# GpSimd takes over one of the two input products of each state step in a fused Mamba, MoE and attention kernel

## The reference

```python
u, z  = split(x @ W_in.T)                       # 256 channels each
uc    = silu(conv3(u) + conv_b)
proj  = uc @ W_xproj.T
B, C, dt = proj[..., :16], proj[..., 16:32], proj[..., 32:]
delta = softplus(dt @ W_dt.T + b_dt)            # per position and channel
for t in positions:                             # state of 256 channels x 16
    h = exp(delta[t] * A) * h + (delta[t] * uc[t]) * B[t]
    y[t] = sum over the 16 states of h * C[t]
out = ((y + uc * D) * silu(z)) @ W_out.T
```

## Time and profile before

| | |
|---|---|
| median of 3 runs | 2798.36 us (2792.71 to 2799.37) |
| the profiled execution, its own time | 2799.84 us |
| its span, first to last instruction | 2797.7 us |
| busy share of the span | PE 77%, DVE 75%, ACT 63%, POOL 55% |
| granted TensorE clock, mean | 0.890 |
| state steps of sequences 0 to 3 | 77 to 905 us of the span |

### The profile page before, as it was taken

One profiled execution on the slowest core, in us unless ns is written; L12 is line 12 of the kernel. 1 busy time (PEld: TensorE's weight loads), 2 busy tenths in 40 slices (PEclk: granted clock), 3 DMA queues, 4 the chain that ended last, 5 costly groups with the idle time before them and its releaser, 6 DMA issues.

```text
span 2797.7 us, 42437 instructions
## 1 busy us (share of the span) xinstructions
PE 2156.8 (77%) x15570; PEld 1468.6 (52%) x15570; DVE 2095.7 (75%) x3549; ACT 1751.3 (63%) x2757; POOL 1549.5 (55%) x1375
## 2 busy tenths in 40 slices
PE   2333787588499597988889898889995798839876
PEld 1101455356266474655666566556664568636665
DVE  3999889789888215999999999999998432572344
ACT  5444776686565546988888888888894234212422
POOL 0435433533533103878877887898788424563146
PEclk8555898799599798999999999999998899859988
DMA  3000000000000000000000010110010000000000
GB/s 109 0 0 0 1 1 1 1 1 1 19 1 1 16 8 23 24 24 24 24 24 24 24 27 23 31 26 24 24 35 24 1 1 1 1 16 1 1 1 16
DMA packets 32032, 42.05 MB, mean 15 GB/s; under 512 B 8897, under 2 KB 18130, under 8 KB 31442
## 3 DMA queue, kind: packets, MB, share of 16 engines
q1 hardware_dynamic: 31826, 39.34, 5.2%
HBM read 12.05 MB, written 2.10 MB: 5 GB/s over the span
## 4 chain that ended last, share of the span: by engine, by line
PE 35%; DVE 29%; ACT 12%; issue 11%; POOL 11%; SPq 0%; DMA 0%; POOLq 0%; ACTq 0%; DVEq 0%
DVE MA L1329 12%; PE ps L891 6%; DVE WB L1338 5%; PE ps L820 3%; POOL MA L429 3%; ACT HR L792 2%; PE ps L1161 2%; PE ps L822 2%; PE ps L821 2%; PE ps L1190 2%; PE ps L2020 2%; ACT BIG L463 2%; PE ps L1173 2%; PE ps L1962 1%; ACT L792 1%
## 5 line engine op out<-in xcount | busy, mean ns | idle before, releaser
L1329 DVE TENSOR_REDUCE MA<-ps 128x1 f32<-128x1024 f32 x512 | 606.6, 1216 | 46.4 <-PE ps L1161 42.5
L1257 ACT ACTIVATE WB<-ps,MA 128x1024 f32<-128x1024 f32 x461 | 513.8, 1118 | 105.5 <-DVE MA L1329 93.3
L429 POOL TENSOR_TENSOR MA<-MA,BIG 128x1024 f32<-128x1024 f32 x128 | 303.0, 2389 | 495.2 <-DVE BIG L355 470.7
L1161 PE MATMUL ps<-BIG 96*128 96x512 f16 x1024 | 315.9, 391 | 98.9 <-ACT WB L1257 87.5
L1413 POOL TENSOR_SCALAR WB<-WB,MA 128x384 f32<-128x384 f32 x256 | 371.1, 1450 | 8.5
L891 PEld LDWEIGHTS ps<-WB,HR 128*128 128x128 f32 x2304 | 279.0, 195 | 27.4 <-issue 11.6
L891 PE MATMUL ps<-WB,HR 128*128 128x128 f32 x2304 | 286.0, 280 | 7.2 <-DVE acc L727 7.2
L792 ACT ACTIVATE HR<-ps,b 128x512 f32<-128x512 f32 x288 | 190.3, 687 | 127.6 <-PE ps L822 126.6
L1767 POOL TENSOR_TENSOR BIG<-MA,BIG 128x512 f32<-128x512 f32 x128 | 133.0, 1048 | 229.5 <-PE ps L2006 76.1
L1173 PE MATMUL ps<-ident,WB 128*128 128x128 f32 x1640 | 223.8, 280 | 9.8 <-DVE WB L1338 5.6
L1416 POOL TENSOR_TENSOR WB<-WB 128x384 f32<-128x384 f32 x205 | 208.9, 1019 | 17.1
(11 more groups left out here) (300 smaller groups left out, 4968.3 us busy)
## 6 DMA issues: line engine op xcount, KB each, us to landing
BIG<-BIG SPq DMA_DIRECT2D x192, 64.0 KB, 2.0
BIG<-MA SPq DMA_DIRECT2D x192, 64.0 KB, 2.0
WB<-w_dram SPq DMA_DIRECT2D x1, 2304.0 KB, 14.7
X<-x_dram SPq DMA_DIRECT2D x4, 512.0 KB, 12.4
HR<-w_dram SPq DMA_DIRECT2D x1, 2048.0 KB, 9.4
out_dram<-X SPq DMA_DIRECT2D x4, 512.0 KB, 3.2
BIG<-wqkv_dram SPq DMA_DIRECT2D x1, 1536.0 KB, 6.2
WB<-w_dram SPq DMA_DIRECT2D x2, 512.0 KB, 4.9
```

The lines of the kernel that those rows point to most:

```text
L429: e.tensor_tensor(yy[:, c, :], yy[:, c, :], db[n % 2][c], ALU.add).then_inc(*p_my.up(b, n, c))
L1161: x = e.matmul(ps[s][:, 512 * h:512 * h + 512], stack[q % 2][0:96, 0, 2 * pp + s, 128 * i:128 * i + 128], stack[q % 2][0:96, 1, 2 * pp + s ...
L1257: e.activation(P_of(n, s), ps[s][:, :], ACT.Exp, bias=L[:, 2 * s + pp:2 * s + pp + 1], scale=1.0, accum_out=L[:, 4 + 2 * s + pp:5 + 2 * s ...
L1329: e.tensor_reduce(L_of(n)[:, c:c + 1], ps[s][:, :], AX, ALU.max, negate=True).then_inc(*v_amx.up(n, s))
```

## The change

Half 0's input product leaves DVE and goes to POOL (inputs_pool), which can't read PSUM, so the row of B is brought by a transfer instead: ACT's queue writes the 16 rows of B from the tile projected to DRAM once per sequence (b_rows), and SP's queue loads row n, spread over 128 partitions (rows_sp), right into db[k][0], where the product is then made in place. scan0 waits for POOL's product (p_mtb), scan1 as before for DVE's. Half 1, both scans, the products with C and POOL's adds stay. The rows0 matmuls stay too, for half 1. DVE's first softplus operation waits for the write of the rows (its output overwrites projected), du of the next sequence waits for POOL's last product of the sequence before. The loads of the attention's weights stand behind rows_sp in SP's queue. Several semaphores are merged into one each (a_mfront, v_mfront) without another order of events, and all planned positions are set anew. Those that the prediction uses, besides LOOP_AT: N_PERIOD 13.11 to 13.1; IN_AT (position in the steps of the sequence before) conv0 92.1 to 96.3, sp0 138.3 to 138.2, dl0 149.4 to 149.5, sp1 161.6 to 161.2, dl1 176.9 to 176.8, stats 61.3 to 61.4 (POOL's scale_shift 2.5 behind it), du 200.1 to 200.

```diff
 LOOP_AT = {"tb": -0.76, "scan1": 2.84, "scan0": 4.1, "th": 7.79, "add": 10.18, ...}     # before
 LOOP_AT = {"tb": -2.59, "scan1": 2.76, "scan0": 5.14, "th": 8.02, "add": 10.55, ..., "tb0": -1.13}  # after
...
         def loop_dve(e, b):
             for n in range(16):
                 k = n % 2
                 yield l_at(b, n, LOOP_AT["tb"])
                 e.wait_ge(*t_mrow[0].at(b, n))
-                for c in range(2):
-                    if n >= 2:
-                        e.wait_ge(*p_my.at(b, n - 2, c))
-                    elif b:
-                        e.wait_ge(*p_my.at(b - 1, 14 + n, c))
-                    e.tensor_tensor(db[k][0] if c == 0 else ps[0][:, :], du[:, c, :], ps[0][:, :], ALU.mult).then_inc(
-                        *v_mtb.up(b, n, c))
+                if n >= 2:
+                    e.wait_ge(*p_my.at(b, n - 2, 1))
+                elif b:
+                    e.wait_ge(*p_my.at(b - 1, 14 + n, 1))
+                e.tensor_tensor(ps[0][:, :], du[:, 1, :], ps[0][:, :], ALU.mult).then_inc(*v_mtb.up(b, n))
                 for c in (1, 0):
                     yield l_at(b, n, LOOP_AT[f"scan{c}"])
                     e.wait_ge(*a_mda.at(b, n, c))
-                    e.wait_ge(*v_mtb.at(b, n, c))
+                    e.wait_ge(*(v_mtb.at(b, n) if c else p_mtb.at(b, n)))
...
+        def inputs_pool(e, b):
+            for n in range(16):
+                yield l_at(b, n, LOOP_AT["tb0"])
+                if n == 0:
+                    e.wait_ge(*v_mtb.at(b, "du"))
+                e.wait_ge(s_bcast[n % 2], 16 * (8 * b + n // 2 + 1))
+                e.tensor_tensor(db[n % 2][0], du[:, 0, :], db[n % 2][0], ALU.mult).then_inc(*p_mtb.up(b, n))
+
+        def rows_sp(e):
+
+            for b in range(NB):
+                e.wait_ge(s_brow, 16 * b + 16)
+                for n in range(16):
+                    if n >= 2:
+                        e.wait_ge(*p_my.at(b, n - 2, 0))
+                    elif b:
+                        e.wait_ge(*p_my.at(b - 1, 14 + n, 0))
+                    e.dma_start(db[n % 2][0], b_dram[b, n:n + 1, :].partition_broadcast(128)).then_inc(s_bcast[n % 2], 16)
...
+            yield in_at(b, "wx", 4.2)
+            e.wait_ge(*a_m.at("wx", b, 1))
+            e.dma_start(b_dram[b, :, :], projected[64:80, :]).then_inc(s_brow, 16)
...
             for c in range(2):
                 yield in_at(b, f"sp{c}")
-                e.wait_ge(*a_mexp.at(b, c))
-                if c:
-                    e.wait_ge(*v_mdl.at(b, 0))
+                e.wait_ge(*a_mfront.at(b, "exp", c))
+                if c == 0:
+                    e.wait_ge(s_brow, 16 * b + 16)
+                else:
+                    e.wait_ge(*v_mfront.at(b, "dl", 0))
...
             yield in_at(b, "du")
+            if b:
+                e.wait_ge(*p_mtb.at(b - 1, 15))
             for c in range(2):
-                e.wait_ge(*v_mdl.at(b, c))
-                e.tensor_tensor(du[:, c, :], dl[b % 2][:, c, :], uc[:, c, :], ALU.mult).then_inc(*dve_own.up())
+                e.wait_ge(*v_mfront.at(b, "dl", c))
+                i = e.tensor_tensor(du[:, c, :], dl[b % 2][:, c, :], uc[:, c, :], ALU.mult)
+                i.then_inc(*(v_mtb.up(b, "du") if c == 0 else dve_own.up()))
...
         @block.gpsimd
-            weave(over(loop_pool, e), over(front_pool, e), over(back_pool, e), over(moe_pool, e),
+            weave(over(loop_pool, e), over(inputs_pool, e), over(front_pool, e), over(back_pool, e), over(moe_pool, e),
...
         @block.sync
         def _(e):
             load(e)
+            rows_sp(e)
             attention_sp(e)
```

More of the change, by code:

```diff
@@ L84, in keys @@
     return out
-N_PERIOD, M_PERIOD, M_FIRST = 13.11, 209.76, 56.0
+N_PERIOD, M_PERIOD, M_FIRST = 13.1, 209.6, 56.0
 PLAN = [(h, e) for h in range(2) for e in (8, 0, 1, 2, 3, 4, 5, 6, 7)]
 WEIGHTED = []
-IN_AT0 = {"stats": -0.58, "norm": 1.89, "tr": 7.85, "u": 12.93, "tap0": 16.6, "tap1": 15.13, "conv0": 14.42,
-          "conv1": 22.1, "silu": 21.6, "wx": 23.8, "bc1": 26.4, "bc2": 27.8, "wdt0": 29.5, "wdt1": 35, "exp": 36.6,
-          "sp0": 40.2, "ln0": 39, "dl0": 42.9, "sp1": 40.1, "ln1": 49.1, "dl1": 51.2, "du": 52.2}
@@ L93 @@
[L93 to L104, removed]
@@ L105 @@
-F_AT3 = {"stats": -0.54, "norm": 3.84, "tr": 1.58, "flo": 14.87, "gate": 11.29, "top": 11.76, "e": 15.6, "wts": 9.85,
-         "cT": 19.46, "k": 13.36, "K": 6.65, "up": 1.05, "dn": 12.94, "dnj": 0.67, "ge": 0.43, "done": -0.33,
-         "add": 7.21, "end": 136.6, "rnorm": 137.1, "x": 135.5}
+IN_AT0 = {"stats": -1.25, "norm": 1.77, "tr": 7.53, "u": 13.01, "tap0": 16.77, "tap1": 12.45, "conv0": 14.68,
+          "conv1": 21.9, "silu": 19.41, "wx": 24.5, "bc1": 28.2, "bc2": 27.5, "wdt0": 29.5, "wdt1": 35.9,
+          "exp": 36.6, "sp0": 40, "ln0": 50.4, "dl0": 43.8, "sp1": 35.7, "ln1": 48.3, "dl1": 50.3, "du": 51.9}
@@ new lines @@
+IN_AT = {"stats": 61.4, "norm": 68.4, "tr": 75, "u": 80.1, "tap0": 89.9, "tap1": 91, "conv0": 96.3, "conv1": 86.7,
+         "silu": 96.6, "wx": 101.5, "bc1": 109, "bc2": 121, "wdt0": 107.6, "wdt1": 126.6, "exp": 135.9, "sp0": 138.2,
+         "ln0": 142.6, "dl0": 149.5, "sp1": 161.2, "ln1": 169.9, "dl1": 176.8, "du": 200}
+OUT_AT = {"gate": 6.92, "yy": 6.94, "out": 11.16, "stats": 18.56, "rstd": 21.2, "norm": 33.2, "x": 35.2}
+OUT_AT3 = {"gate": 1.22, "yy": 7.14, "out": 5.72, "stats": 7.8, "rstd": 19.15, "norm": 13.22, "x": 22.4}
@@ new lines @@
+F_AT0 = {"stats": -2.31, "norm": 5.53, "tr": 6.58, "flo": 8.97, "gate": 10.05, "top": 17.5, "e": 15.83, "wts": 11.99,
+         "cT": 25.8, "k": 17.92, "K": 8.73, "up": 0.87, "dn": 3.66, "dnj": 1.45, "ge": 1.19, "done": 11.03,
+         "add": 8.31, "end": 181.3, "rnorm": 190.6, "x": 186.4}
+F_AT2 = {"stats": 3.93, "norm": 2.49, "tr": 6.54, "flo": 14.29, "gate": 18.14, "top": 23.4, "e": 24, "wts": 26.6,
+         "cT": 26.5, "k": 17.67, "K": 8.28, "up": 0.65, "dn": 6.97, "dnj": 0.23, "ge": 0.92, "done": 11.15,
+         "add": 8.32, "end": 176, "rnorm": 170.2, "x": 179.4}
@@ L108 @@
+F_AT3 = {"stats": -0.61, "norm": 1.25, "tr": 1.84, "flo": 15.09, "gate": 11.25, "top": 10.63, "e": 15.89,
+         "wts": 10.09, "cT": 19.39, "k": 13.36, "K": 6.65, "up": 1.04, "dn": 7.56, "dnj": 0.57, "ge": 0.46,
+         "done": -0.09, "add": 6.98, "end": 137.5, "rnorm": 137.1, "x": 135.6}
 F_AT = [F_AT0, F_AT0, F_AT2, F_AT3]
-LOOP_AT = {"tb": -0.76, "scan1": 2.84, "scan0": 4.1, "th": 7.79, "add": 10.18, "da": -0.17, "rows0": 5.17,
-           "rows1": 13.83, "z": 18.68, "zK": -4.54, "za": 4.8}
@@ L111 @@
-A_AT = {"norm0": 10.66, "norm1": -0.24, "norm2": 10.19, "turn": 9.1, "op": 15.77, "opK": 2.47, "ope": 0.85,
-        "v": 36.5, "vK": -3.75, "lam": -12.29}
+LOOP_AT = {"tb": -2.59, "scan1": 2.76, "scan0": 5.14, "th": 8.02, "add": 10.55, "da": 0.03, "rows0": 5.28,
+           "rows1": 13.84, "z": 19.93, "zK": -1.57, "za": 6.24, "tb0": -1.13}
+A_AT = {"norm0": 10.44, "norm1": -0.26, "norm2": 8.64, "turn": 8.51, "op": 15.77, "opK": 2.47, "ope": 1.65,
+        "v": 40.8, "vK": -5.27, "lam": -12.29}
@@ L235, in program @@
             path[p], user[n] = (x, user.get(n)), p
-        a_muc, a_mexp, a_mlog, a_mda = tick("a_muc", NB, 2), tick("a_mexp", NB, 2), tick("a_mlog", NB, 2), tick("a_mda", NB, 16, (1, 0))
-        a_myy, a_mtap = tick("a_myy", NB, 2), tick("a_mtap", NB, 2)
+        a_mfront, a_mda = tick("a_mfront", NB, ("tap", "silu", "exp", "log"), 2), tick("a_mda", NB, 16, (1, 0))
+        a_myy = tick("a_myy", NB, 2)
         t_mrow = {k: tick(f"t_mrow{k}", NB, 16) for k in range(2)}
@@ L241, in program @@
         v_mst, a_mln, p_mrs = (Tick(sem(x), m_order) for x in ("v_mst", "a_mln", "p_mrs"))
-        v_mconv, v_mbc, v_mu1, v_mdl = tick("v_mconv", NB, 2), tick("v_mbc", NB), tick("v_mu1", NB, 2), tick("v_mdl", NB, 2)
-        v_mtb, v_mscan, v_mth = tick("v_mtb", NB, 16, 2), tick("v_mscan", NB, 16, (1, 0)), tick("v_mth", NB, 16, (1, 0))
+        v_mfront = Tick(sem("v_mfront"), [(b, x, c) for b in range(NB) for x, c in (("conv", 0), ("conv", 1), ("bc", 0), ("u1", 0), ("dl", 0),
+                                                                                ("u1", 1), ("dl", 1))])
+        v_mtb, v_mscan, v_mth = tick("v_mtb", NB, ("du", *range(16))), tick("v_mscan", NB, 16, (1, 0)), tick("v_mth", NB, 16, (1, 0))
         v_mgate = tick("v_mgate", NB, 2)
+        p_mtb, s_brow, s_bcast = tick("p_mtb", NB, 16), sem("s_brow"), [sem(f"s_bcast{k}") for k in range(2)]
+        b_dram = nc.dram_tensor("b_rows", (NB, 16, 1024), F32, kind="Internal").ap()
         p_my, p_mx = tick("p_my", NB, 16, (1, 0)), tick("p_mx", NB)
@@ L515, in front_act @@
                 e.wait_ge(*a_m.at("wdt", b, c, 1))
-                e.activation(ee[c], ee[c], ACT.Exp, bias=0.0, scale=-1.0).then_inc(*a_mexp.up(b, c))
+                e.activation(ee[c], ee[c], ACT.Exp, bias=0.0, scale=-1.0).then_inc(*a_mfront.up(b, "exp", c))
             for c in range(2):
                 yield in_at(b, f"ln{c}")
-                e.wait_ge(*v_mu1.at(b, c))
```

(3 more changed lines are left out.)

34 lines of the change are left out of this document (17 added, 17 removed).

## The result

The changed kernel takes 2838.54 us (median of 4, 2833.55 to 2847.33) against 2798.02 (median of 4, 2792.71 to 2799.37): a ratio of 1.0156, with the interval 1.014 to 1.0172. It is 40 us slower. The forecast was 2815 in a range that ends at 2838: slower, as forecast, but by more than twice as much, and just outside the range.

A forecast was written before the change was run, and what follows sets the result against it. DVE was taken to bound sequence 0's steps, the experts on PE and ACT to set the pace in the other stages. 2799.84 + 18.0 - 1.1 + 0 = 2816.7 us, against the median 2815; range 2777 to 2838.

The forecast's parts named there:

- Bare periods: Steps without other work, in sequence 0: from 9.08 us to 10.54 us each, 1.46 us longer.
- the sum for sequence 0: Sequence 0's 16 periods, taken one by one: plus 18.0 us, hidden by nothing.
- the ring: Between DVE and POOL: th, two adds, next step's product, scan0, th again, waiting on each other, 10.54 us a step.
- Two engines at one port: DVE operations with two SBUF inputs and POOL operations go one after the other; without it, 3 us less in sequence 0.
- Loads: Row loads of 512 KB, write of 64 KB and later attention weights: all hidden, cost 0.
- Stages of sequences 1 to 3: Steps beside the experts: gains and losses cancel, 0 taken, with -18 and +8 us as ends for each.
- Outside of it I reckon ... 0 to +2: Sequences 1 to 3, periods outside PE's and ACT's chain: 0 to +2 us per stage.
- The +1 for gate and statistics: Sequences 1 to 3: gate and back statistics, 2.3 us each, lie behind scan0; +1 us per stage.
- The other moved positions ... 3 us to either side: Remaining moved positions and merged semaphores, not priced from rows: 3 us to either side.
- The rival with the dearer port: Front and back two-input operations wait for whole POOL operations in sequences 1 to 3: 8 us a stage, 2839; 0.08 together with late loads.
- Freed DVE time is worth nothing where PE and ACT carry the chain: Sequences 1 to 3, periods of 13 to 22 us: a DVE done sooner just waits longer for PE.
- The rival with 54 us to come back: Freed DVE time returns in the three expert stages: two thirds, 36 us, gives 2779; chance 0.27.

The follow-up runs named there:

- the port alone: Kernel before, plus one extra POOL product per step of sequence 0, behind the two adds, that no step waits for: sequence 0 takes 188.4 us.
- old positions: Changed kernel with all planned positions of the kernel before: 2835.8 us, ratio 1.0138 to the kernel before.
- the run with steps 8 to 14: Kernel before's positions, with POOL making half 0's product only in steps 8 to 14 of sequences 1 to 3: 2797.02 us, ratio 0.9997.
- the last version: Kernel before, with POOL's product ahead of the adds and a third buffer in sequence 0's steps 1, 3, 6, 10, and later convolution there: 2796.57 us, ratio 0.9995.
- the run with the third buffer: Changed kernel with a third buffer for half 0 in sequence 0 and the next step's product ahead of the adds: 2818.9 us.

## Why the prediction was right and wrong

- **Bare periods and the sum for sequence 0**: right. 10.54 us, and 188.9 - 170.8 = 18.1 for the stage against 18.0; the first scan0 1.7 us earlier against 1.1. Most parts are right within a microsecond: the statistics period 13.28 (13.1), sp0 12.42 (12.4), dl1 12.92 (12.9), convolution 14.95 (15.6), the B and C pairs in the gap 12.06 and 11.89 (11.7). Two errors cancel: sp1 (offset 161.2) stands ahead of scan0 of step 12 and so in dl0's period, which takes 14.28 us, and leaves the next one bare, 10.53; I had 12.9 and 11.7. du has the right number, 12.87 (12.8), for another reason: it isn't held by the port (2.36 us for its two operations) but stands idle for 2.41 us, waiting for POOL's last product. I named the ring as the cause and the port as an addition to it; the port alone makes 188.4, so that the sum would have come out without the ring.
- **Two engines at one port**: right, also in the part for which there was no row (the earlier trace rows is not the only such place before: at 722 us scan0 takes 4.13 and the adds 6.63 us again). In the changed kernel's timeline a cast, with one input, comes due 0.04 us ahead of the product, and another time, in sequence 2's steps, 0.69 us behind it:

```profile
164.61 0.69 DVE L377 CAST rows<-lnb 96x1024 bf16<-96x1024 f32 x1
164.65 2.86 POOL L431 TENSOR_TENSOR BIG<-MA,BIG 128x1024 f32<-128x1024 f32 x1
165.33 3.25 DVE L379 TENSOR_TENSOR lnb<-lnb,rows 64x1024 f32<-64x1024 f32 x1
...
620.64 2.35 POOL L431 TENSOR_TENSOR BIG<-MA,BIG 128x1024 f32<-128x1024 f32 x1
621.33 2.20 DVE L377 CAST rows<-lnb 96x1024 bf16<-96x1024 f32 x1
```

The first time the product takes 2.86 instead of 2.35 us, held until the cast is done, and the next operation, with two inputs, 3.25 instead of 1.22. The second time the cast takes 2.20 instead of 0.69: it ends 0.5 us behind the product (623.53 and 622.99). By the Trainium skill's rule ("SBUF — State Buffer", section "SBUF: two separate sides") the cast takes the lock as well, and the trace agrees in both orders. The period with the first cast is 12.06 us, between my 11.7 and the 12.4 with the cast waiting for the whole product; here the product waited.
- **Loads**: right, 3.6 us, hidden.
- **Stages of sequences 1 to 3**: the step that failed. I took 0, with -18 to +8 for each; they lost 12.5, 6.6 and 3.4, together 22.5 us. The profiled execution is 18.9 us above its forecast (2835.61 against 2816.7): 22.5, less 3 behind the last scan0 and 0.6 at the first. Two terms were wrong. "Outside of it I reckon ... 0 to +2" was mis-sized: periods 0 to 5 lost 10.1, 5.6 and 2.3 (old positions: 9.7, 6.5, 4.3). In sequence 1 all six got longer, none shorter by the 1.1 that DVE is freed of. The +1 for gate and statistics was +1.6 and +3.0 there: these periods grew from 11.36 and 11.29 to 12.96 and 14.25. My own rule, that work behind scan0 lengthens the ring by its full length, would have given it. The statistics period, between scan0 at 277.55 and the next:

```profile
281.97 2.32 DVE L355 TENSOR_TENSOR BIG<-BIG,ps 128x1024 f32<-128x1024 f32 x2
...
284.75 4.65 POOL L453 TENSOR_TENSOR MA<-MA,BIG 128x1024 f32<-128x1024 f32 x2
...
291.80 4.34 DVE L349 TENSOR_TENSOR_SCAN BIG<-BIG 128x1024 f32<-128x1024 f32 x1 [3.98 <-POOL BIG L431]
```

  The statistics put off th by 2.2 us, and POOL's scale_shift, which waits for them, puts off the adds by another 1.5 (284.75 instead of 281.97 + 1.27): 10.54 + 2.2 + 1.5 = 14.25. Nor did I price that the experts' own scale stands behind the product on POOL and comes 7.4 us later (44.2 instead of 36.8 us after the first scan0); put first, it gave back 2.5 us in sequences 1 and 2 each. That is on the chain of PE and ACT that I had called the bound. Behind periods 0 to 5 (+18.0 in all) period 6 adds 11.5 us and the periods from 7 on give back 7.0; this part is less firm, as the last section shows. "The other moved positions ... 3 us to either side" was too narrow: by themselves they cost 7 at the last scan0, +4.2 and +6.7 in sequences 1 and 2.
- **The rival with the dearer port** said 2839, and 2838.54 was measured, but not by its mechanism. It wanted 8 us a stage from front and back operations on DVE that wait for POOL. In sequences 1 to 3 of the changed kernel DVE operations run 11.1 us longer in all than the shortest of their kind (scan0 at 291.80 2.1, the second operation of sp1 2.0 twice, the cast 1.5, two small ones 3.4), before for 5.5: 5.6 us more, not 24.
- **Freed DVE time is worth nothing where PE and ACT carry the chain**: right, shown by the run with steps 8 to 14. The rival with 54 us to come back had nothing behind it.
- **Open**: how product and positions share the loss in sequences 1 to 3. Apart they give 15.8 and 9.5 us, together 22.5, and single periods differ by more than that beside a different clock (below). I did not try the changed kernel with everything replanned around the scale.

## What to carry to other kernels

Taking 1.1 us a step off a busy engine bought nothing, because the operation came to an engine that holds up, and is held up by, scan0: GpSimd's 4.7 us and the scan's 2.2 fitted into a period of 9.1, GpSimd's 7.0 and 2.2 fill it, and standing just where scan0 comes due they made it 10.3 to 10.5. Most of that was the place: with the product ahead of the adds and a third buffer the mean was 8.7, and 3 of the 18 us of the stage were left. Before moving work to GpSimd, add up per period all its operations and all VectorE operations with two SBUF inputs, and look which of them will meet. Where another stage's chain passes through the receiving engine in a few places (here scale, addition to x, scale), look what the new work stands in front of: here a product of 2.35 us made the scale 4.1 us later.

## What the runs showed of the hardware that I had not expected

The same stretch of the experts ran at different clocks in profiled executions of kernels that differ by a few microseconds ahead of it. Windows of 10 us from some 20 us ahead of period 6 of sequence 1 into it (it starts at 320.3, 346.9, 344.0 and 321.7 us), columns as in the earlier trace rows (the granted clock is the seventh value behind the window, 0.50 is the lower of the two levels, 1.2 GHz, 1.00 the higher, 2.4 GHz). Before:

```profile
300.00:310.00 10.00, 6.55 (x27) 2.70 (x28) 9.76 (x29) 9.27 (x12) 6.44 (x4) 0.83 0.00 0
310.00:320.00 10.00, 10.00 (x69) 7.60 (x69) 9.90 (x7) 7.96 (x16) 5.32 (x5) 1.00 0.00 0
```

The changed kernel:

```profile
325.00:335.00 10.00, 5.99 (x26) 2.57 (x24) 8.18 (x21) 8.67 (x11) 8.15 (x7) 0.84 0.13 52
335.00:345.00 10.00, 10.00 (x36) 7.14 (x34) 7.07 (x5) 4.11 (x10) 6.42 (x4) 0.50 0.00 0
345.00:355.00 10.00, 10.00 (x49) 7.21 (x49) 3.28 (x2) 5.59 (x8) 1.78 (x1) 0.69 0.17 54
```

With the scale ahead of the product:

```profile
325.00:335.00 10.00, 7.19 (x28) 3.20 (x26) 6.85 (x18) 9.43 (x15) 8.02 (x7) 0.73 0.17 52
335.00:345.00 10.00, 10.00 (x69) 7.61 (x68) 7.39 (x6) 6.42 (x12) 6.98 (x3) 1.00 0.16 52
345.00:355.00 10.00, 9.89 (x50) 5.76 (x50) 5.84 (x8) 8.57 (x12) 4.12 (x2) 1.00 0.01 2
```

And the last version, whose sequence 1 has nothing changed in its steps:

```profile
300.00:310.00 10.00, 6.32 (x21) 2.17 (x22) 9.76 (x29) 9.41 (x12) 6.27 (x4) 0.69 0.00 0
310.00:320.00 10.00, 10.00 (x35) 7.37 (x34) 8.77 (x7) 3.89 (x10) 5.48 (x5) 0.50 0.00 0
320.00:330.00 10.00, 9.07 (x48) 6.21 (x47) 3.96 (x2) 6.54 (x9) 0.00 (x0) 0.79 0.01 2
```

In the first and third PE comes to the full load of the down products at 1.00 and does 69 matmuls in 10 us; in the second and fourth it comes there at 0.50, does 36 and 35 in the same fully busy 10 us and gets the higher clock only in the next window (0.69 and 0.79 in the mean). An up product of the same size takes 379 ns in the first and third and 634 in the others. Ahead of it PE is busy for 5.99 to 7.19 of 10 us in all four, with pauses between the expert block's first products. Period 6 follows: 23.7 and 22.4 us with the higher clock, 28.9 and 29.9 with the lower. The run with the moved scale is 6.5 us shorter there for a start 4 us earlier, and the last version, 2.6 us shorter in sequence 0, is 6.2 longer in period 6 of sequence 1. What tips it these runs don't show, nor how much of each period's difference is the clock and how much the other start; but a difference of some 5 us in this period stands beside a different clock each time.

Nor do they show that it belongs to the version and not to the one execution that was profiled. The last version's was 6.6 us above its own median. And the run with the third buffer, which in sequences 1 to 3 is the changed kernel, had 69 matmuls at 1.00 from 321 to 331 us and took 21.0 us in period 6 of sequence 1, where the changed kernel took 28.9; from there on it gave most of it back (145.3 against 147.7 us from period 6 on). So a single profile tells little about a single period here; sums over a stage and medians of several executions tell more.
